# Masking the score maxima on VectorE instead of TensorE, with an earlier start of batch 0's maxima, in a two-layer attention and expert kernel

## The reference

```
x = x + tanh(g_xattn[0]) * L0_xattn(layernorm(x), ctx)   # 16 heads of 16, causal
x = x + tanh(g_ffn[0])   * L0_ffn(layernorm(x))          # 32 experts, top 8, capacity 256, F 192
x = x + tanh(g_xattn[1]) * L1_xattn(layernorm(x), ctx)   # 16 heads of 16, no causal mask
x = x + tanh(g_ffn[1])   * L1_ffn(layernorm(x))          # 8 experts, top 2, F 1024
# attention:
scores = einsum('bhqd,bhkd->bhqk', wq, wk) / sqrt(16)
scores = where(causal, scores, finfo.min)                # L0 only
out = einsum('bhqk,bhkd->bhqd', softmax(scores), wv)
```

## Time and profile before

| | |
|---|---|
| runs of the kernel | 1954.91, 1957.07, 1960.56 us, median 1957.07 |
| the profiled execution | 1959.72 us; span 1958.0 us |
| PE busy | 1784.8 us, 91% |
| DVE / ACT / POOL busy | 1006.0 / 887.7 / 788.7 us |
| granted TensorE clock | 0.97 of full speed on average |
| steady iteration of attention 0 | 57.4 us per batch (first scores 82.10, end of the last about 535) |
| stage limits | attention 0 to 581, experts 0 to 828, attention 1 to 1460, experts 1 to 1958 |

### The profile page before, as it was taken

One profiled execution on the slowest core, in us unless ns is written; L12 is line 12 of the kernel. 1 busy time (PEld: TensorE's weight loads), 2 busy tenths in 40 slices (PEclk: granted clock), 3 DMA queues, 4 the chain that ended last, 5 costly groups with the idle time before them and its releaser, 6 DMA issues. The chain is left out here.

```text
span 1958.0 us, 31351 instructions
## 1 busy us (share of the span) xinstructions
PE 1784.8 (91%) x11109; PEld 1094.3 (56%) x11109; DVE 1006.0 (51%) x2638; ACT 887.7 (45%) x1684; POOL 788.7 (40%) x772
## 2 busy tenths in 40 slices
PE   7799999999858999588999999999967999999997
PEld 5456656665547777443344444433344766766675
DVE  4656666677556444238677777777521222212211
ACT  4466666665603222155777778766731111111110
POOL 4211667766626777531114124211133134433323
PEclk9999999999969999799999999999988999999999
DMA  5554555643317887444333343231132133333314
GB/s 163 164 180 152 149 162 151 178 109 117 113 44 188 167 176 166 80 142 134 110 107 111 103 131 106 81 119 52 55 104 93 21 80 87 85 81 83 73 29 133
DMA packets 210331, 224.10 MB, mean 114 GB/s; under 512 B 40048, under 2 KB 200818, under 8 KB 209511
## 3 DMA queue, kind: packets, MB, share of 16 engines
q1 hardware_dynamic: 176490, 177.54, 30.1%
q0 software_dynamic: 33408, 44.69, 12.1%
q10 hardware_dynamic: 288, 0.00, 0.0%
HBM read 156.14 MB, written 87.06 MB: 124 GB/s over the span
## 5 line engine op out<-in xcount | busy, mean ns | idle before, releaser
L1001 DVE TENSOR_REDUCE nmx<-mxb 128x1 f32<-128x512 f32 (+2 forms) x866 | 502.2, 609 | 249.6 <-PE mxb L737 128.5
L838 ACT ACTIVATE pt<-stb 128x512 f32<-128x512 f32 x832 | 474.0, 600 | 247.7 <-PE stb L753 120.6
L734 PE MATMUL mxb<-kst,qst 96*128 96x512 bf16 (+2 forms) x986 | 318.4, 344 | 18.3 <-DVE nmx L1001 14.7
L753 PE MATMUL stb<-qst,kst 99*128 99x512 bf16 (+4 forms) x1024 | 326.7, 342 | 5.8 <-DMA qst<-m3T 3.3
L769 PE MATMUL ob<-pt,va 128*32 128x512 f32 (+3 forms) x2048 | 219.4, 523 | 2.5 <-ACT pt L838 1.7
L753 PEld LDWEIGHTS stb<-qst,kst 102*128 102x128 bf16 (+1 forms) x1024 | 99.4, 98 | 214.4 <-ACT pt L838 130.7
L1358 POOL DMA_INDIRECT slots<-number,place x192 | 189.3, 986 | 58.6 <-issue 58.5
L1328 POOL TENSOR_TENSOR qk<-qk,parts 128x512 f32<-128x512 f32 x60 | 68.5, 1165 | 314.2 <-ACT qk L877 204.4
L1897 POOL DMA_INDIRECT x_after_l<-e_y,e_token x56 | 87.2, 1558 | 242.7 <-DVE e_y L1862 229.3
L734 PEld LDWEIGHTS mxb<-kst,qst 99*128 99x128 bf16 (+1 forms) x986 | 96.7, 98 | 118.1 <-DVE nmx L1001 58.1
L1650 POOL DMA_INDIRECT x_after_l<-e_y,token x64 | 102.5, 1601 | 50.4 <-DMA x_after_l<-e_y,token 23.2
(11 more groups left out here) (280 smaller groups left out, 3013.9 us busy)
## 6 DMA issues: line engine op xcount, KB each, us to landing
kst<-qk_parts SPq DMA_DIRECT2D x384, 64.0 KB, 2.3
qst<-qk_parts SPq DMA_DIRECT2D x384, 64.0 KB, 2.3
qk_parts<-parts SPq DMA_DIRECT2D x14, 1536.0 KB, 6.5
rows<-rows SPq DMA_DIRECT2D x15, 1060.0 KB
crow<-in_ctx SPq DMA_DIRECT2D x16, 512.0 KB, 4.0
x_after_l<-xres SPq DMA_DIRECT2D x16, 512.0 KB, 3.3
e_gu_nat<-in_L_ffn_gate_up_proj SPq DMA_DIRECT2D x64, 128.0 KB
qst<-in_L_ffn_w SPq DMA_DIRECT2D x8, 1024.0 KB, 6.7
```

The source lines that it names most:

```text
L734: last = pe.matmul(out, qst[par][0:rows_used, h, qt * P:(qt + 1) * P], kst[par][0:rows_used, h, 0:nk], start=True, stop=not causal)
L753: last = pe.matmul(bank[:, to:to + S - q_from(kt)], kst[par][0:ROWS, h, kt * P:(kt + 1) * P], qst[par][0:ROWS, h, q_from(kt):S], start=Tru ...
L838: act.activation(pt[:, slot(b, u), q0:S], stb[no % N_ST][:, q0:S], ACT.Exp, scale=SCALE).then_inc(s["st_free"], 1)
L1001: last = dve.tensor_reduce(nmx[:, qt, h:h + 1], got[:, at:at + k_to(qt)], AX.X, ALU.max, negate=True)
```

## The change

Four edits stand in one diff.

1. In layer 0 the mask matmuls (L737) go. `hide_max` grows from 128 to 512 columns, and DVE adds it and takes the maximum in one operation, `tensor_tensor_reduce`, for each head and query tile, with the result in `nmx` by its accumulator. The reduces of two heads in one instruction become one per head. As the new operation does not negate, the first step of `shift_part` multiplies by -1.
2. Batch 0's maxima are spread by a new function `filling` over both filling iterations (5 banks at u = 8 of iteration -2, 10 more there from u = 24, 36 over iteration -1). The `qst` half of batch 0's group 0 is issued by ACT, and so is `shift(0, 0)`. This holds for both layers.
3. At the end of attention 0, the one-hots, list matmuls and `enlist` of batch 6 stand late in iteration 8, and the list has a bank of its own (`stb[0]`). "n" of the second half changes from bank 1 to bank 0 (both layers).
4. The indirect transfers of the experts of layer 0 carry no bounds, and of expert 0 the rows are transposed behind its weights.

```diff
-    c.hide_max = sb(c, ctx, "hide_max", [P, P], BF16)
+    c.hide_max = sb(c, ctx, "hide_max", [P, S], BF16)
...
-    18: ("list", -2, 0, 0, 0), 20: ("list", -2, 0, 1, 0), 25: ("list", -2, 0, 2, 0), 28: ("list", -2, 0, 3, 0),
-    8: ("o", -1, 3, 0, 1), 9: ("k", 2, 1, 0, 0), 11: ("n", -1, 0, 0, 1), 12: ("k", 2, 1, 1, 0), 13: ("n", -1, 1, 0, 1),
+        8: ("o", -1, 3, 0, 1), 9: ("k", 2, 1, 0, 0), 11: ("n", -1, 0, 0, 1), 12: ("k", 2, 1, 1, 0), 13: ("n", -1, 1, 0, 0),
...
+AHEAD = 5
+FILLED = AHEAD + 10
...
-ONE_HOT_AT = (1, 4, 6, 7, 9, 10, 12, 14, 19, 20, 21, 22, 23, 24, 25, 26)
+ONE_HOT_AT = {6: (30, 30, 31, 31, 32, 32, 33, 33, 34, 34, 35, 35, 36, 36, 37, 37),
+              7: (1, 1, 2, 2, 3, 3, 4, 4, 5, 5, 6, 6, 7, 7, 8, 8)}
+LIST_AT = {6: (32, 34, 36, 38), 7: (2, 4, 6, 8)}
+ENLIST_AT = {6: 38, 7: 9}
...
+        def filling(it, u):
+            if it == -2:
+                return range(0, AHEAD) if u == 8 else range(AHEAD + (u - 24) // 4, AHEAD + (u - 23) // 4) if u >= 24 else ()
+            if it == -1:
+                share = STEPS - BEHIND - FILLED
+                return range(FILLED + share * u // STEPS, FILLED + share * (u + 1) // STEPS)
+            return ()
...
+                    if side == 0 and n == 0 and g == 0:
+                        continue
...
-                if nxt == 0:
-                    shift(nxt, 0)
...
+            def list_(b, part):
+                n = b - LISTED
+                if part == 0:
+                    wait(pe, evac["list"], n)
+                    pe.wait_ge(s["st_free"], N_SCORE * B)
+                pe.wait_ge(s["lo_rdy"], 4 * n + part + 1)
+                for k in range(8):
+                    last = pe.matmul(stb[0][:, N_HI * part:N_HI * (part + 1)], lo1[part % 2][:, k, :], hv[part % 2][:, k, :],
+                                     start=k == 0, stop=k == 7)
...
-                                     start=True, stop=not causal)
-                    if causal:
-                        last = pe.matmul(out[:, nk - P:nk], c.identb[:, :], c.hide_max[:, :], start=False, stop=True)
+                                     start=True, stop=True)
...
+                if n == 0 and hf == 0:
+                    act.wait_ge(evac["shift"], 1)
+                    for r in range(3):
+                        act.dma_start(qst[0][ROW_SHIFT + r:ROW_SHIFT + r + 1, 0:HALF, :],
+                                      m3T[0][HALF * r:HALF * (r + 1), :]).then_inc(s["shift_in0"], 16)
...
+            act.wait_ge(s["parts_out"], 16)
+            for r, term in enumerate(Q_TERM):
+                act.dma_start(qst[0][DH * r:DH * r + DH, 0:4, :],
+                              qk_dram[0][0, term].rearrange("(h d) s -> d h s", d=DH)[:, 0:4, :]).then_inc(stack_in[0][0], 16)
...
-                (h, qt, _), *others = MAX_BANKS[u]
-                if others and others[0][1] == qt:
-                    last = dve.tensor_reduce(nmx[:, qt, h:h + 2], got[:, 0:2 * k_to(qt)].rearrange("p (h k) -> p h k", h=2),
-                                             AX.X, ALU.max, negate=True)
-                else:
-                    for h, qt, at in MAX_BANKS[u]:
+                for h, qt, at in MAX_BANKS[u]:
+                    if causal:
+                        last = dve.tensor_tensor_reduce(got[:, at:at + k_to(qt)], got[:, at:at + k_to(qt)], c.hide_max[:, S - k_to(qt):S],
+                                                        op0=ALU.add, op1=ALU.max, scale=1.0, scalar=HIDDEN, accum_out=nmx[:, qt, h:h + 1])
+                    else:
                         last = dve.tensor_reduce(nmx[:, qt, h:h + 1], got[:, at:at + k_to(qt)], AX.X, ALU.max, negate=True)
...
-                                            bass.IndirectOffsetOnAxis(token[:, TILES * e + i:TILES * e + i + 1], 0),
-                                            bounds_check=T + CAP0 - 1, oob_is_err=True).then_inc(rows_in[e % N_ROW], 16)
+                                            bass.IndirectOffsetOnAxis(token[:, TILES * e + i:TILES * e + i + 1], 0)).then_inc(rows_in[e % N_ROW], 16)
```

More of the change, by code:

```diff
@@ L630, in bank_free @@
                     pe.wait_ge(evac[before], value)
-                held[bank] = (kind, PER_ITEM[kind] * (b - LISTED if kind == "list" else b) + t + 1)
+                held[bank] = (kind, PER_ITEM[kind] * b + t + 1)
             def trip(kind, b, t, part):
@@ L703, in trip @@
                                                  start=i == NT and ii == 0, stop=ii == i - 1)
-                elif kind == "list":
-                    pe.wait_ge(s["lo_rdy"], 4 * (b - LISTED) + part + 1)
-                    for k in range(8):
-                        done = pe.matmul(out[:, N_HI * part:N_HI * (part + 1)], lo1[part % 2][:, k, :], hv[part % 2][:, k, :],
-                                         start=k == 0, stop=k == 7)
                 else:
@@ L715, in trip @@
                     done.then_inc(full[kind], 1)
+            def list_(b, part):
[7 more added lines that the diff above has]
+                                     start=k == 0, stop=k == 7)
+                last.then_inc(full["list"], 1)
             def maxima(n, u):
@@ L809, in _ @@
                         maxima(cur, u + STEPS - BEHIND)
-                    if u >= BEHIND and nxt is not None:
+                    if u >= BEHIND and nxt:
                         maxima(nxt, u - BEHIND)
+                    for first_u in filling(it, u):
+                        maxima(0, first_u)
                     for call, at in enumerate(sorted(VALUE_CALLS)):
@@ L816, in _ @@
                             values(cur, (u - at) // 16, call)
+                    if layer == 0 and LISTED <= it - 2 < B and u in LIST_AT[it - 2]:
+                        list_(it - 2, LIST_AT[it - 2].index(u))
                     if u in TRIPS:
@@ L821, in _ @@
                             keep({"n": 10, "p": 10 * (t == 0), "y": 90 * (t == 0), "lg": 10}.get(kind, 0), mxb[0])
-                        if item(it, k) is not None and (kind != "list" or layer == 0 and item(it, k) >= LISTED) and (kind not in FRONT or item(it, k) > 0):
+                        if item(it, k) is not None and (kind not in FRONT or item(it, k) > 0):
                             trip(kind, item(it, k), t, part)
@@ L1011, in shift_part @@
                     dve.wait_ge(link, at)
-                cast = dve.tensor_copy(m3[hf][:, :, r, :], nmx[:, :, heads])
+                if causal and r == 0:
+                    cast = dve.tensor_scalar(m3[hf][:, :, r, :], nmx[:, :, heads], -1.0, None, ALU.mult)
+                else:
+                    cast = dve.tensor_copy(m3[hf][:, :, r, :], nmx[:, :, heads])
                 if r == 2:
@@ L1231, in _ @@
                 for u in range(STEPS):
-                    if layer == 0 and it == -2 and u == 14:
+                    if layer == 0 and it == -2 and u == 6:
                         set_up_bias()
@@ L1526, in _ @@
             turn(0)
+            turn_rows(0)
             for e in range(E0):
```

38 lines of the change are left out of this document (27 added, 11 removed).

## The result

The changed kernel takes 1974.14 us (median of 4, 1973.59 to 1975.57), the kernel before 1957.66: ratio 1.008, 95% interval 1.0064 to 1.0095. It is slower by 0.8%, where a gain of 1.4% was forecast. The profiled execution has a span of 1972.9 us against 1958.0, 14.9 more.

The account below looks back on a forecast made before the run. TensorE was taken to bound attention 0, GpSimd layer 0's experts, VectorE layer 1's fill. Terms -16.5 - 7 - 8 + 1.5 + 6 - 5 = -29 gave 1928 us against the median 1957.1, stated as 1930, range 1906 to 1952.

Parts of the forecast that it names:

- the tail: End of attention 0: the last list matmul holds up the 90 matmuls and y, +6 us (ends +2, +8).
- Queued behind ACT's new wait is its normalisation for x(1): Layer 0's fill: batch 1's normalisation follows ACT's wait; x(1) moves by 4 to 5 us, fill still -7 us.
- part 2: The two pipeline fills: -7 us in layer 0 (ends 0, -9) and -8 us in layer 1 (ends -2, -10).
- ACT now issues these in parallel, 2.8 us earlier: Layer 0's fill: group 0's last transfers, issued by SP from 32.23 to 35.00 before, should have landed by about 35.
- 7 x 3.8 = -27 us, if nothing takes PE's place: Attention 0's body: 64 mask matmuls of 0.06 us off TensorE save 3.8 us per batch, over 7 batches.
- part 1: Mask moved to VectorE in attention 0's body: -27 + 7 + 2 + 1.5 = -16.5 us (ends -25, -6).
- r: VectorE's cost of each of 64 second instructions per batch in attention 0: taken as 0.13 us, between 0.07 and 0.26.
- some 0.3 us in each of 5 iterations: n's second half in bank 0 waits for ACT's evacuation: 1.5 us in attention 0, as much in layer 1.
- The bounds: Layer 0's experts: transfers without bounds save 0.04 us each in POOL's issue, -5 us (from nothing to at most 20).
- which bounds don't change: End of layer 0's experts: each add's wait of 3.06 us for the one before stays as it was.
- the fills give nothing: Rival: the maxima in front hold batch 1's set-up in the fills, 1930 + 15 = 1945 us; chance 0.12.
- The rival on the slower side, VectorE as bound: Attention 0: the new operation needs two passes, 68 us per batch, +75 us in 7 batches, 2030 us; chance 0.11.

Follow-up runs that it names:

- number 5: Changed kernel with batch 0's first five banks of maxima and the bias set-up put back behind batch 1's statistics: 1955.9 us, 0.9965 of the kernel before.
- a_best: Changed kernel, statistics first, list's old places, n in bank 1, four slot transfers moved, layer 1's batch 0 maxima at old steps: 1944.3 us, 0.9937 of the kernel before.
- best2: Changed kernel with statistics first in layer 0, list's old places, n in bank 1, layer 1's whole fill as before: 1941.4 us, 0.9907 of the kernel before.
- number 13: Kernel before without any mask in layer 0's maxima and with every second transfer to the slots left out: ratio 0.9912, steady period 59.43 us.
- 11: Kernel before with layer 0's mask on VectorE and every second transfer to the slots left out: ratio 0.9959, steady period 60.03 us.
- number 1: Kernel before with only the mask of layer 0's maxima moved to VectorE: 1954.3 us, ratio 0.9967.
- number 3: Kernel before with only the second half of n moved from bank 1 to bank 0, both layers: 1964.8 us, ratio 1.0028.
- number 6: Changed kernel with batch 6's one-hots, list matmuls and addition back at their old steps: 1967.2 us, 1.0024 of the kernel before.
- number 4: Kernel before with only the bounds taken off the 128 indirect transfers of layer 0's experts: 1950.0 us, ratio 0.9949.
- 8: Changed kernel with statistics first in the fill, the list's old places and n back in bank 1: 1941.7 us, 0.9888 of the kernel before.
- 2: Kernel before with no mask at all in layer 0's maxima, VectorE working as before: 1950.0 us, ratio 0.9954.
- b_half: Kernel before with every second transfer to the slots left out, mask still on TensorE: ratio 1.0022, steady period 62.72 us.
- b_spread: Kernel before with four of a batch's 32 GpSimd transfers to the slots moved earlier: ratio 1.0024, period 62.7 us.
- m_spread: Kernel before with the mask on VectorE and four of a batch's 32 slot transfers moved earlier: ratio 0.9952, period 60.4 us.

## Why the prediction was wrong

The measured span is 44 us off the forecast (+14.9 against -29). The two fills missed by 34 us and the two bodies by 18; the experts gave 7.5 more than forecast and the tail was right within 1.

**The step that failed first: "Queued behind ACT's new wait is its normalisation for x(1)" in part 2.** The fill was followed on TensorE, on ScalarE's queue and on SyncE's, but not on VectorE. There the reduces of batch 0's first banks, moved with the matmuls that feed them, stand in front of batch 1's statistics and inherit the wait for group 0; in layer 0 the moved set-up of the biases stands there too. x of batch 1 was put 4 to 5 us behind its 31.86 and came at 46.11. Of the 34 us (-7 and -8 forecast, +7.8 and +11.3 measured) number 5 gives 19 back: first scores 10.4 us earlier in layer 0, and 8.5 less from last add to first scores in layer 1. How the 10.4 divide between banks and biases no run shows.

**"ACT now issues these in parallel, 2.8 us earlier" failed next.** ACT's issue waits for the second store; it was through at the same time as SP's in layer 0 and started no earlier in layer 1, while its wait and its six issues (3.9 to 4.4 us in layer 0, 2.7 in layer 1) stand ahead of the normalisation. With the maxima at their old places the issue by ACT, shift included, costs layer 1's fill 7.4 us (a_best against best2). With the statistics first, layer 1's fill is 2.8 us longer than before where 8 less were forecast, and layer 0's 2.5 us shorter where 7 were. What is left of that in layer 0 no run took apart.

**"7 x 3.8 = -27 us, if nothing takes PE's place" in part 1.** 3.84 us per batch was right for the matmuls' own time: TensorE is busy 60.29 us of the steady batch of 61.60 before and 56.89 of 61.30 after. VectorE's price was over-estimated: the second instruction costs nothing measurable by itself, the two together 0.05 us more than a reduce, where r was taken as 0.13, and 0.60 us per batch in the period (number 13 against 11). The condition did not hold: waits took TensorE's place, and for a part of them the reason is GpSimd. The earlier trace rows had it at 40.10 of 57 us, which does not look like a limit; but each of its transfers has 0.30 us of issue around it that is not counted as busy. POOL in one steady batch after (300.24 to 361.54 us):

```profile
L1398 POOL DMA_INDIRECT slots<-number,place x32 | 31.4, 980 | 9.7 <-issue 9.7
```

32 transfers of 1.28 us, eight operations of 1.16 and the two normalisations, near 3 us, make near 54 us of a period of 61, in one order, with waits for ScalarE between them. That order was nowhere in the sum. Thinned out it gives 0.9 us per batch; what remains are TensorE's waits for VectorE's maxima and for ScalarE, which grew as the mask went, and why they fall as they do is not shown. So of the body's forecast 16.5 us, 4.5 came in number 1 (449.6 from first scores to first `keep`, 0.7 per batch in the steady part), and 3.2 in the changed kernel, where n's bank and the lower clock take a part back.

**n's bank, "some 0.3 us in each of 5 iterations".** The mechanism was right and its size was off: 1.14 us per batch in layer 1 (number 3), in each of the first four of the seven periods from y to y. The wait itself is 0.92 us there. In layer 0 n waits some 0.7 us per batch in number 3 (3.4 us in 344), but p behind it waits 1.0 instead of 3.6, and the period grows by 0.4 only.

**The tail** was right, +6 forecast and +4.9 measured, by the mechanism given (number 6).

**The bounds** were right in direction; -5 forecast, -9 measured alone (some 7 to 9, by the spread of that stretch). The sum placed the saving in the 0.30 of issue, 0.04 for each of four transfers. The steady period did fall by 0.14 us per expert, 4.5 in all, but in the durations of the two gathers; issue and adds are as long as before. That the steady period came out at the forecast's size is luck. What it missed is in "which bounds don't change": the wait of an add for the one before it fell from 3.06 to 2.54, and TensorE's wait for gathered rows from 16.4 to 8.5 us in number 4.

**The rivals.** That the fills give nothing was given 0.12 and a price of 15 us; what happened is this rival with more than twice its price (34 us), by another mechanism. The rival on the slower side, VectorE as bound, did not occur: VectorE was busy 44.07 of 61.30 us. Its 2030 is also 10 us more than its own terms give (1957 - 12.5 + 75). The 57.4 us per batch, and with it the 53.6 to which VectorE's need was compared, is the mean named above and not the period.

## What to carry to other kernels

When work is moved, follow the operations that consume it too, on each in-order engine: a reduce that goes along with its matmul takes its wait in front of whatever stands behind it there. An engine's busy share does not include its issue gaps; add them before calling an engine free, and take the period from one batch to the next, not a mean with the ends. And work taken off the engine with 97% busy time is worth its length only as far as the waits between the engines allow: here 0.7 of 3.84 us per batch, and 1.6 with GpSimd's chain thinned out.

## What the runs showed that was not expected

**The clock can fall after less than 2 us of waiting, and does not each time.** In the changed kernel TensorE waited 1.34 and 0.44 us at 268, and 1.33 and 0.44 at 331. Behind the first wait its matmuls of 128 columns start 0.11 us apart (270.37, 270.48), behind the second 0.06 apart: these are its two clock levels, 1.2 and 2.4 GHz. The timeline of PE, then busy times in 10 us windows at both places (the clock is the third number from the right):

```profile
270.37 0.31 PE L769 MATMUL stb<-qst,kst 102*128 102x128 bf16 x1
270.48 0.31 PE L772 MATMUL stb<-hide_st,identb 128*128 128x128 bf16 x1
...
333.10 0.22 PE L769 MATMUL stb<-qst,kst 102*128 102x128 bf16 x1
333.16 0.22 PE L772 MATMUL stb<-hide_st,identb 128*128 128x128 bf16 x1
```

```profile
270.00:280.00 10.00, 8.98 (x51) 4.69 (x50) 5.21 (x25) 5.30 (x11) 5.96 (x8) 0.83 0.33 73
...
330.00:340.00 10.00, 7.47 (x48) 4.22 (x49) 6.72 (x31) 8.08 (x15) 7.00 (x8) 1.00 0.52 109
```

The granted clock of 270 to 280 us reads 0.83, and the batch that holds it took 62.97 us where its neighbours took 60.95 and 61.30. Such batches, some 1.3 to 2.1 us over the others, also stand in runs 1, 8 and 15 (one each) and 2 and 6 (two each), each with 0.83 in a window of 10 us. The kernel before has a clock of 1.00 from 110 to 470 us, and so have b_half, b_spread, m_spread and n_half. The last two wait as much as the changed kernel (22.7 and 20.5 us in 344, against 22.8), so that the sum of the waits does not decide it; what does is not shown. So a wait on the busiest engine can cost more than its length; a reading of 0.83 over 10 us is 1.7 us of full clock, an estimate of its price in one batch, and a part of the gain that the mask did not bring.
